# A graph layer on one core: TensorE's picking products put in front of the sums in each step

## What is computed

```python
h = jnp.maximum(_layernorm(x, axis=-1), 0.0)
x_i, x_j = h[dst], h[src]
tmp = jnp.concatenate([x_i, x_j, edge_attr], axis=1)   # 48 + 48 + 32
z = jax.nn.relu(tmp @ W1 + b1)                         # 128 wide
msg = z @ W2 + b2                                      # 48 wide
return x + jax.ops.segment_sum(msg, dst, num_segments=12500)
```

## Time and profile before

| | us |
|---|---|
| median of 3 runs | 3468.96 |
| lowest, highest | 3467.29, 3474.36 |
| span of the profiled execution | 4774.3 |
| TensorE busy in it (matmul) | 3927.4 |
| GpSimd busy in it | 2613.2 |
| VectorE busy in it | 2554.6 |
| ScalarE busy in it | 2043.4 |

### The profile page before, as it was taken

One profiled execution on the slowest core, in us unless ns is written; L12 is line 12 of the kernel. 1 busy time (PEld: TensorE's weight loads), 2 busy tenths in 40 slices (PEclk: granted clock), 3 DMA queues, 4 the chain that ended last, 5 costly groups with the idle time before them and its releaser, 6 DMA issues.

```text
span 4774.3 us, 95161 instructions
## 1 busy us (share of the span) xinstructions
PE 3927.4 (82%) x21992; PEld 3397.9 (71%) x21992; DVE 2554.6 (54%) x5906; ACT 2043.4 (43%) x7414; POOL 2613.2 (55%) x2766
## 2 busy tenths in 40 slices
PE   3788888888888888888888888888888888888887
PEld 3677777777777777777777777777777777777776
DVE  3655555565555555555555555555555555555553
ACT  2444444444444444444444444444444444444443
POOL 5455555555555555555555555555555555555555
PEclk9988888888888888888888888888888888888886
DMA  4522222222222222222222222222222222222223
GB/s 146 142 80 72 75 78 79 78 78 75 76 77 76 78 74 75 76 78 76 76 75 74 77 77 77 76 76 73 77 74 77 75 77 73 78 75 79 74 79 81
DMA packets 286658, 380.47 MB, mean 80 GB/s; under 512 B 90916, under 2 KB 190549, under 8 KB 285542
## 3 DMA queue, kind: packets, MB, share of 16 engines
q0 software_dynamic: 88064, 177.91, 14.7%
q1 hardware_dynamic: 198342, 201.58, 14.6%
q10 hardware_dynamic: 208, 0.49, 0.1%
HBM read 362.58 MB, written 17.04 MB: 80 GB/s over the span
## 4 chain that ended last, share of the span: by engine, by line
another core or an unknown queue 30%; issue 19%; DVE 18%; PE 14%; DVEq 11%; SPq 4%; ACT 4%; DMA 1%; ACTq 0%
PE ps L1310 6%; DVEq L1004 5%; DVE lhs L992 5%; PE ps L1286 3%; PE ps L1294 3%; DVE gath L1001 2%; DVE work L1047 2%; DVE onehot L979 2%; DVE p_hot L1025 2%; ACT work L674 2%; DVE nodes L1014 2%; SPq L411 1%; SPq L412 1%; DVEq L1093 1%
## 5 line engine op out<-in xcount | busy, mean ns | idle before, releaser
L535 POOL DMA_INDIRECT gath<-b_table,idx x2688 | 2549.3, 948 | 2127.3 <-ACT idx L639 1294.6
L1310 PE MATMUL ps<-h_tab,p_hot 128*128 128x480 f32 (+1 forms) x6768 | 1944.0, 431 | 259.5 <-issue 255.7
L1310 PEld LDWEIGHTS ps<-h_tab,p_hot 128*128 128x128 f32 x6768 | 1449.9, 226 | 467.6 <-issue 344.3
L674 ACT ACTIVATE work<-ps,work 128x80 f32<-128x80 f32 x4136 | 1039.1, 408 | 1675.3 <-remote 1458.2
L1286 PE MATMUL ps<-rhs,lhs 96*128 96x128 f32 x5376 | 906.6, 316 | 270.1 <-DVE gath L1001 124.3
L1286 PEld LDWEIGHTS ps<-rhs,lhs 96*128 96x128 f32 x5376 | 785.3, 219 | 403.1 <-issue 331.8
L1014 DVE TENSOR_TENSOR nodes<-ps,nodes 48x48 f32 x768 | 153.7, 200 | 1611.5 <-remote 1490.1
L1294 PE MATMUL ps<-onehot,gath 128*128 128x48 f32 x5376 | 799.6, 295 | 88.4 <-ACT gath L655 75.0
L1294 PEld LDWEIGHTS ps<-onehot,gath 128*128 128x128 f32 x5376 | 783.1, 221 | 109.1 <-ACT gath L655 95.0
L1025 DVE TENSOR_TENSOR p_hot<-work,ps 128x1152 fp32r<-128x1152 f32 x376 | 506.6, 1347 | 57.7 <-PE ps L1310 34.0
L992 DVE TENSOR_SCALAR_CACHE_REDUCE lhs<-nodes 48x512 f32<-48x512 f32 (+1 forms) x768 | 520.0, 677 | 32.0 <-issue 5.7
(11 more groups left out here) (128 smaller groups left out, 1640.8 us busy)
## 6 DMA issues: line engine op xcount, KB each, us to landing
nodes<-dst_row SPq DMA_DIRECT2D x494, 96.0 KB
gath<-b_table,idx POOLq DMA_INDIRECT x2688
nodes<-dst_row SPq DMA_DIRECT2D x384, 72.0 KB
lhs<-in_edge_t SPq DMA_DIRECT2D x384, 64.0 KB
work<-key_row SPq DMA_DIRECT2D x94, 256.0 KB
lhs<-in_edge_t SPq DMA_DIRECT2D x384, 48.0 KB
rhs<-a_table SPq DMA_DIRECT2D x768, 24.0 KB
work<-in_edge_t SPq DMA_DIRECT2D x220, 32.0 KB
```

The source lines that it names most:

```text
L535: pool.indirect_dma_start(gath[:, u, t, :], None, b_table, bass.IndirectOffsetOnAxis(ap=idx[:, u, t:t + 1], axis=0)).then_inc(gathered[u], 16)
L674: m = nc.scalar.activation(p_sel[:, t % 2, :, at_j], ps_run[:, q, j * words:(j + 1) * words], ACT.Copy, scale=p_mask[:, at_j, t:t + 1])
L1310: mm = nc.tensor.matmul(ps_run[:, q, 0:m * words].rearrange("p (j w) -> p j w", j=m), p_hot[:, t % 2, i, :], h_tab[:, first:first + BLOCKS ...
```

## The change

In each step of all cycles but the last, TensorE runs `run_p(j)` right after `make_z(k - 1)`, in front of `make_sums(k - 3)` and of the tail's parts. No instruction is added or removed, no wait is changed, and the lists of the other engines stay as they are.

```diff
                 for j in range(PERIOD + EXTRA if final else PERIOD):
                     k = LEAD + c * PERIOD + j
                     make_z(k - 1, it)
+                    if not final:
+                        run_p(j, c, it)
                     make_sums(k - 3, it)
                     if j == 3 and ends_e:
                         make_sums_tail(place_e(c - 1, it))
...
                     if j == 7 and c < EARLY:
                         turn_e(c, it)
-                    if not final:
-                        run_p(j, c, it)
                     if j % 2 == 0:
                         fold(k - 3, it)
```

## The result

The changed kernel takes 3481.05 us (median of 5 runs, 3479.84 to 3481.84), before 3468.54: a ratio of 1.0036, 95% interval 1.0025 to 1.0047. It is slower, by 12.5 us and not by the 131 of the forecast (3600, range 3490 to 3710).

The account below looks back on a forecast made before the run. The prediction took TensorE as the bound, with 3370 us of its own time; 188 us of fold waits made 3558, and under half of the 99 us idle staying gave 3600 us (+3.8%), range 3490 to 3710.

Parts of the forecast that it names:

- the fold that loses its cover: TensorE's fold in even steps waits for ScalarE's copy of the sums: 0.50 us each, 376 folds, +188 us (124 to 226).
- late indices: Sums 2.15 or 1.72 us later release GpSimd's indices later; about 5 us of slack, so costed at nothing.
- the sums' wait for the relu: TensorE's make_sums waits for ScalarE's relu, 52 places, 75 us when profiled; it goes, worth 0 to 75 us.
- TensorE is the bound of an ordinary run, 97% full: TensorE needs 3370 us of the median 3469, at most about 99 us of it idle or slow.
- Some 170 us lie around it: TensorE's time outside the loops, from first make_z at 165.8 us and last fold at 4770.3 of 4774.3.
- The pair at 7.69 us: Pure TensorE work of a pair of steps without the tail product, 8.57 - 0.88; 376 such pairs make 2891 us.
- at most 1.23 us: GpSimd's true pace per gather, lowered from 1.25 because 2688 gathers from 154 us on gave 3514, above the median.
- rival 1: The fold's stall fills TensorE's idle time, GpSimd's gathers set the time: 3469 us, no change; chance 0.09.
- Rival 2: GpSimd starves as indices come 2 us later: 4220 us, or 3790 for a quarter plus the fold; chance 0.05.
- Rival 3: Faster: the relu wait is worth its whole 75 us and copies hide, 3432 us at 0.10 a fold; chance 0.06.
- Rival 4: TensorE's clock falls to 0.50 for one step in each cycle: 169 us on top, 3770; chance 0.06.
- the weight load that might be pulled over a wait: TensorE's queue might pull the fold's first load ahead, leaving 0.33 us a fold, 124 us; judged unlikely from the trace.

Follow-up runs that it names:

- e1_before: The kernel before, unchanged, profiled once more for a trace to lay beside the changed kernel's; 3468.33 us.
- e5: The kernel before with one gather fewer in every 4-tile step of the loops, part of the output wrong; 3228.12 us, 0.9289 of before.
- e3: Kernel before with the change in even steps only (480 columns, fold after the sums), odd steps as before; 3517.22 us, ratio 1.0148 to before.
- e2: The changed kernel with each fold, tails' folds too, one place later, behind make_z of the following odd step; 3468.75 us, ratio 1.0003 to before.

## Why the prediction was wrong

**The way and the mechanism at the fold were right**: slower, by the fold that loses its cover, 0.45 us of weight-load wait in 380 places (8 of them old) for the 0.50 in 376. Also right: late indices cost GpSimd nothing, the tails nothing (in the original balance), the sums' wait for the relu goes, and ScalarE is at hand for the copy.

**The step that failed is the first one, "TensorE is the bound of an ordinary run, 97% full".** In e1_before it is busy for 3231 us (93%) and waits besides; alone it needs 3228 us (e5), not 3370. Two terms were too large:

- The lead. "Some 170 us lie around it" came from the first make_z at 165.8 us. In the trace of after it is at 101.6 us, and about 106 us lie around the loops. The trace on record was disturbed in the front too, and I had distrusted it only for idle time: 64 us.
- The pair at 7.69 us. e5 has 8.29 - 0.88 = 7.41. The difference is in two distances of the earlier trace rows, make_z of 3 tiles 0.84 us (0.67 in e5) and make_sums of 3 tiles 0.69 (0.59); the others agree within 0.01. The matmul rows of the stretch show no wait in brackets, but the weight loads, which I left out, do: the sums waited for the relu there. 376 x 0.28 = 105 us.

```profile
230.50 0.74 PEld L1294 LDWEIGHTS ps<-onehot,gath 128*128 128x128 f32 x6 [0.20 <-ACT gath L655]
```

3370 - 64 - 105 = 3201, within 1% of the 3228 measured.

**The contradiction that could have told.** The prediction worked out that the gathers need 3514 us by the trace, more than the run lasts, and put this down to their pace ("at most 1.23 us"). The pace was right: 1.249 us. The start was wrong: 154 for 95. 95 + 2688 x 1.249 = 3452, and 15 us for the end and the first waits make the 3468 to a few us. With GpSimd as the bound the forecast would have been rival 1, to which I gave 0.09. The 12 us need more than the bound: the cycles have to be counted apart, since two tails in a cycle decide which engine is the longer one there, where I had spread 110 tails evenly over 384 pairs; and the pair has to be 7.41. Then a cycle has 4 x 7.41 + 2.53 = 32.2 us with one tail and 34.7 with two, and 4 x 0.33 more after the change: 33.5 and 36.0 against 34.97, so some 16 x 1.0 us. With my 7.69 and 0.50 even the later cycles would have come out over 34.97 (35.3).

**The price of the fold** was 0.50 us for a net of 0.33: the stall itself was right, the gain of other neighbours in the new order was not looked for. This did not decide the outcome: with a pair of 7.41 a later cycle stays below GpSimd's 34.97 us at either price (34.2 at 0.50).

**The rivals.** Rival 1 is what happened in 77 cycles out of 94: GpSimd's gathers set the time. Its condition, a TensorE 5% faster than traced, was not needed: the pair was 3.6% shorter, and the rest was the lead. Rival 2 did not come: GpSimd's wait for indices is 46 us in 138 places in after, on average no more than its ordinary gap. Rival 3 had no ground, the relu's wait being 10 us before. Rival 4 did not come in this kernel: the mean granted clock is 0.99 in both orders, and with 372 short waits more the clock of after fell only once in the loops, for 3.4 us. It did come in e3, 12 times for some 7 us, though that has only half of the edit. There the clock fell at 459.6 us with no wait of TensorE over 0.52 us in the 13 us before, where the prediction had it fall only after long stops. The Trainium skill, "TensorE: Matmul & The Clock Gate", on the second failure mode, says that in one kernel frequent short idle moments between groups of matmuls made the clock swing between its two levels; e3 and e2 agree with that, after hardly does, and no run shows what tells them apart. On the weight load that might be pulled over a wait the trace agrees with the earlier trace rows: the fold's load waits 0.45 us.

## What to carry to other kernels

Work out each engine's time in the loop for itself, at its own pace with its fixed gaps, and for every kind of cycle apart: the sum with the larger total is the bound, and added time on another engine is free up to the difference, cycle by cycle, as long as no other chain moves: e3, with the same stalls, cost four times as much, by waits for ScalarE and a falling clock. If an engine's sum comes out longer than the run, one of its terms is wrong; find out which before choosing a bound, and take starts as well as paces from a trace only if its span agrees with an ordinary run, and look at the weight loads before calling a stretch free of waits. An instruction moved between a producer and a consumer on one in-order engine is a cover; moving it away costs the consumer's round trip (0.50 us here, of which new neighbours gave back 0.17) as soon as that engine is the bound.

## What the runs showed of the hardware that was not expected

- GpSimd is the bound with a busy share of 75%: a gather is 0.94 us, and 0.30 us pass before the next one can start, though nothing is waited for. TensorE, the busiest engine of the page at 93%, is not.
- A stall on a busy engine can hide: 168 us of new waits on TensorE, 92% busy, cost 12.5 us.
- The granted clock of TensorE can fall in one order of the same instructions and not in another: 12 stretches of some 7 us at 0.50 in e3, one of 3.4 us in the loops of after.
- The order of independent rows of matmuls changes their own time by some hundredths of a microsecond at each border: make_z is followed by the products after 0.91 us and by the sums after 0.99.
- One profiled execution of before took 4774.3 us, and another of the same kernel 3466.7; in the longer one the front was stretched as well (first gather at 154 for 95 us). A pair of steps without a visible stop took 3.4% longer (8.57 for 8.29 us), all of it at two starts, one of them a wait that only the weight loads show.
